# Eight-layer hybrid model on one Trainium2 core: attention divided inside its own block, and all products of the fast-weights layer on VectorE

## What is computed

```python
# a: alibi attention, 4 sequences of 1024 tokens, 16 heads of 8 values
scores = einsum('bqhd,bkhd->bhqk', q, k) / sqrt(8) + slopes * -abs(i - j)
X += einsum('bhqk,bkhd->bqhd', softmax(scores), v) @ Wout + bout
# m0: mixture of 8 experts, twice:  z += sum_e combine_e * w2_e(silu(w1_e rms(z)))
# b: the same attention with another bias:  scores = q k / sqrt(8) * decay ** abs(i - j)
# m1: the experts again
# f: fast weights, 16 heads of 64, 4 steps of the recurrence over 1024 columns
q = elu(q) + 1; k = elu(k) + 1; q /= sum(q); k /= sum(k); beta = sigmoid(beta)
for k_t, v_t, q_t, b_t in steps:
    W = W + (b_t * (v_t - W k_t))[:, None] * k_t[None, :]
    out = W q_t
h = layer_norm(h + out @ W_o)
# l0: lora ffn      c: centred attention, softmax(xc xc^T) x, no weights      l1: lora ffn
```

## Time and profile before

| what | us |
|---|---|
| median of 3 runs (3472.40 to 3484.07) | 3475.57 |
| the profiled execution, and its span | 3491.22, 3489.5 |
| attention a: projection, the block, normalise, project_out | 15.8 to 89.7, 94.7 to 586, to 603, to 616.4 |
| m0 | 617.8 to 1118.8 |
| attention b: the same four | 1121.6 to 1209.7, 1215.7 to 1705.9, to 1723, to 1737 |
| m1 | 1738.6 to 2240.1 |
| f: norm, dots, values, norm | 2243 to 2264.5, 2265.8 to 2557.3, to 2770.6, to 2805.6 |
| l0 | 2806.6 to 2856 |
| attention c: split, the block, normalise | 2857.9 to 2916.5, 2922.7 to 3402, to 3420 |
| l1 | 3421.2 to 3478.9 |

### The profile page before, as it was taken

How to read it: one execution, slowest core, us unless ns; L and a number is a source line. 1 busy time by engine, 2 the same in 40 slices (tenths; PEclk the granted TensorE clock), 3 DMA queues, 4 the chain that set the end, 5 groups by cost and what they waited for, 6 DMA issues and landing times. The chain is left out here.

```text
span 3489.5 us, 54163 instructions
## 1 busy us (share of the span) xinstructions
PE 2953.6 (85%) x18300; PEld 1343.2 (38%) x18300; DVE 2203.5 (63%) x3764; ACT 2352.7 (67%) x3403; POOL 411.4 (12%) x245
## 2 busy tenths in 40 slices
PE   4888888899998498898899999787868656999997
PEld 2221223566665211111356666522236441111116
DVE  5777777677776777777767777677789862000004
ACT  5789987555454699999655544464624447999992
POOL 2000000000000400000000000065634320000002
PEclk8899999999999799999999999899979867999996
DMA  5433441000000634333100000000000004222210
GB/s 121 57 53 50 59 59 20 25 0 1 0 0 5 171 48 55 53 52 49 29 6 0 1 0 0 26 1 0 0 0 0 0 14 99 41 41 37 42 29 27
DMA packets 68365, 111.08 MB, mean 32 GB/s; under 512 B 10656, under 2 KB 22944, under 8 KB 67312
## 3 DMA queue, kind: packets, MB, share of 16 engines
q1 hardware_dynamic: 68176, 108.58, 18.4%
HBM read 80.85 MB, written 27.69 MB: 31 GB/s over the span
## 5 line engine op out<-in xcount | busy, mean ns | idle before, releaser
L1660 ACT ACTIVATE m_mix_hidden<-m_mix_up_ps 128x512 f32<-128x512 f32 x512 | 305.5, 597 | 294.5 <-PE m_mix_up_ps L1604 294.5
L935 ACT ACTIVATE b_direct_probs<-b_direct_s_ps 128x1024 f32<-128x1024 f32 x512 | 473.6, 1094 | 14.3 <-PE b_direct_o_ps L883 11.7
L1612 PE MATMUL m_mix_down_ps<-m_w,m_mix_hidden 128*128 128x128 f32 x4096 | 474.8, 276 | 0.0
L935 ACT ACTIVATE c_att_probs<-c_att_s_ps 128x1024 f32<-128x1024 f32 x512 | 470.3, 1219 | 5.9 <-PE c_att_o_ps L883 4.1
L1612 PEld LDWEIGHTS m_mix_down_ps<-m_w,m_mix_hidden 128*128 128x128 f32 x4096 | 467.2, 192 | 15.3 <-issue 15.3
L1604 PE MATMUL m_mix_up_ps<-m_mix_ZT,m_w 128*128 128x512 f32 x1024 | 470.5, 617 | 0.3 <-ACT m_mix_hidden L1660 0.3
L935 ACT ACTIVATE a_direct_probs<-a_direct_s_ps 128x1024 f32<-128x1024 f32 (+10 forms) x512 | 431.5, 939 | 56.1 <-DVE a_direct_s_ps L964 42.2
L964 DVE SCALAR_TENSOR_TENSOR a_direct_s_ps<-distance,slopes,a_direct_s_ps 128x512 f32<-128x512 f32 (+3 forms) x512 | 355.4, 732 | 121.8 <-PE a_direct_s_ps L863 119.1
L961 DVE TENSOR_TENSOR b_direct_s_ps<-b_direct_s_ps,distance 128x512 f32<-128x512 f32 x512 | 336.0, 695 | 141.1 <-PE b_direct_s_ps L863 140.8
L950 DVE COPY c_out_t<-c_att_o_ps 128x512 f32 x32 | 22.1, 692 | 465.4 <-PE c_att_o_ps L883 465.2
L883 PE MATMUL b_direct_o_ps<-b_direct_probs,v_cols 128*32 128x512 f32 x2048 | 274.4, 608 | 14.1 <-DVE b_out_t L950 13.1
(11 more groups left out here) (330 smaller groups left out, 3511.7 us busy)
## 6 DMA issues: line engine op xcount, KB each, us to landing
qk_parts<-b_qkv_parts SPq DMA_DIRECT2D x48, 256.0 KB, 3.1
qk_parts<-a_qkv_parts SPq DMA_DIRECT2D x24, 256.0 KB, 3.6
a_k_rows<-qk_parts SPq DMA_DIRECT2D x32, 192.0 KB
a_q_rows<-qk_parts SPq DMA_DIRECT2D x32, 192.0 KB
b_k_rows<-qk_parts SPq DMA_DIRECT2D x32, 192.0 KB
b_q_rows<-qk_parts SPq DMA_DIRECT2D x32, 192.0 KB
qk_parts<-c_split_parts SPq DMA_DIRECT2D x24, 256.0 KB, 3.0
c_k_rows<-qk_parts SPq DMA_DIRECT2D x32, 192.0 KB
```

Source lines behind the costliest of these rows:

```text
L935: act.activation(probs[:, J % 2, j, lo:hi], s_ps[:, slot(hg, n), lo:hi], ACT.Exp).then_inc(exped, 1)
L1612: last = pe.matmul(down_ps[:, t % 2, e, :], hidden[:, e * HALVES + h, t * P:(t + 1) * P], w["w2"][:, e * HALVES + h, :], start=(h == 0), s ...
L1660: act.activation(hidden[:, f, :], up_ps[:, f % UP_BANKS, :], ACT.Silu).then_inc(silu_done, 1)
```

## The change

**Attention.** `out_t` is gone. `take_sums` copies into `taken`, with room for two groups. SyncE moves each group's results by four DMAs of 8 rows x 1024 to `joined` (heads on partitions, tokens along) and the sums of its four heads to DRAM. Once a batch is complete, its 16 x 1024 sums are read back as a dense 128x128 (`gather`), VectorE inverts them (`invert`), SyncE writes them (`keep`) and reads them spread over 128 partitions, 512 KB (`spread_out`), and VectorE multiplies the batch's 128x1024 (`scale`). In VectorE's order, `invert` stands after unit 24 of group 1, `scale` after unit 24 of group 3, of the batch that follows. The loads for a group now wait for the third exponential of the group before the coming one instead of for its takes, and stand ahead of the moves in SyncE's queue. The last group is treated apart: TensorE spreads its sums (`spread_sums`), VectorE divides on the spot (`divide`), and its product with `Wout` comes as a second matrix product into the same bank. The output projection (`finish`) is part of the block: eight groups of four products, six of them copied by ScalarE and added to `X` by GpSimd, the last two added by VectorE. The bias of the output is added by GpSimd after each batch. `normalise` is gone from all three layers; the old `project_out` remains in another form in a branch that is not taken with these inputs.

**Dots.** The two halves become 16 rounds in a row, without a loop. All products are VectorE's, in eight pieces, one after each take. The sums of the first half are copied, turned (into a PSUM bank of their own) and stored during rounds 8 to 11.

**Values.** The products of steps 1 and 2 are VectorE's too (`weigh`), with one buffer each instead of two, and the adds to `H` are put in another order.

The core of the diff:

```diff
-def attend_transposed(nc, tag, V, operands, out_t, ident, table=None, slopes=None, span=None):
+def attend_transposed(nc, tag, V, operands, joined, ident, table=None, slopes=None, span=None, X=None, w_out=None,
+                      b_out=None, kept=None):
+    SCALE_AT = 24
+    EARLY = 2 * (BATCH - 1)
+    KNOWN = (HG - 1) * GH * HD
+    FINISHED = (0, 1, 2, 3, EARLY, 4, 5, EARLY + 1)
...
+            def move(b, hg, past=0):
+                sp.wait_ge(o_out, b * (2 * HG) + (2 * hg + 6 - past * 2 * HG))
+                at = bass.ds(b * SEQ - past * SEQ, SEQ)
+                for j in range(GH):
+                    to = slice((hg * GH + j) * HD, (hg * GH + j + 1) * HD)
+                    sp.dma_start(joined[to, at], taken[VW * j:VW * j + HD, hg % 2, :]).then_inc(moved[hg % 2], 16)
+                sp.dma_start(sums_dram[bass.ds(b * HEADS + (hg * GH - past * HEADS), GH), :],
+                             taken[HD:P:VW, hg % 2, :]).then_inc(sums_kept[hg % 2], 16)
...
             def ahead(b, hg):
-                sp.wait_ge(o_out, b * (2 * HG) + (2 * hg + 2))
+                sp.wait_ge(exped, b * NB + ((hg - 1) * UNITS + SLOTS))
                 operands.load(sp, hg % HG, b + hg // HG)
...
+            def batch(b, first, final):
                 for hg in range(1, HG + 1):
-                    ahead(b, hg)
+                    if not (final and hg == HG):
+                        ahead(b, hg)
+                    if hg >= 2:
+                        move(b, hg - 2)
+                    elif not first:
+                        move(b, HG - 1, 1)
+                    if not first and hg >= 2:
+                        (gather, keep, spread_out)[hg - 2](b)
...
+            def scale(b, last=0):
+                dve.wait_ge(moved[0], b * (2 * MOVES) + 2 * MOVES)
+                dve.wait_ge(moved[1], b * (2 * MOVES) + (2 - last) * MOVES)
+                dve.wait_ge(spread, b * 16 + 16)
+                n = (HEADS - last * GH) * HD
+                out = joined[0:n, bass.ds(b * SEQ, SEQ)]
+                dve.tensor_tensor(out, out, inverse[0:n, :], ALU.mult).then_inc(scaled, 1)
+            def divide(c):
+                dve.wait_ge(sums_spread, c + 1)
+                held = taken[:, (HG - 1) % 2, c * BANK:(c + 1) * BANK]
+                dve.reciprocal(o_ps[:, c, :], o_ps[:, c, :]).then_inc(spread_inverted, 1)
+                dve.wait_ge(spread_inverted, c + 1)
+                dve.tensor_tensor(held, held, o_ps[:, c, :], ALU.mult).then_inc(divided, 1)
...
+                        if not first and n == SCALE_AT and hg == 1:
+                            invert(b - 1)
+                        if not first and n == SCALE_AT and hg == HG - 1:
+                            scale(b - 1)
+                            if final:
+                                invert(b, 1)
...
-    POOLS = (("kk", 1), ("kq", 0), ("kq", 1), ("kq", 3))
-    DVES = (("kk", 2), ("kk", 3), ("kq", 2))
+    PIECES = (("kk", 1, 0, 1), ("kq", 0, 0, 1), ("kq", 1, 0, 2), ("kk", 2, 0, 2), ("kk", 3, 0, 3), ("kq", 2, 0, 3),
+              ("kq", 3, 0, 2), ("kq", 3, 2, 4))
+    PIECES_AFTER = ((0, 1), (2,), (3,), (4,), (5,), (6,), (7,), ())
+    TURN_AT = {(FT8 + 1, 3): 0, (FT8 + 2, 1): 1, (FT8 + 2, 7): 2}
...
+            for r in range(ROUNDS):
+                for u in range(UNITS):
+                    take(r, u)
+                    if r:
+                        for piece in PIECES_AFTER[u]:
+                            multiply(r - 1, piece)
+                    if (r, u) in STORE_AT:
+                        store(0, STORE_AT[r, u])
...
-                    for t, prod in ((1, prod1), (2, prod2)):
-                        pool.wait_ge(v_out, b * STEPS + (t + 3))
-                        pool.tensor_tensor(heads(prod[:, half, :, :]), heads(v[:, half, 0:t + 1, :]),
-                                           of_tile(b, t, t + 1), ALU.mult).then_inc(scaled, 1)
...
+                def weigh(t, prod):
+                    dve.wait_ge(v_out, b * STEPS + (t + 3))
+                    dve.tensor_tensor(heads(prod[:, :, :]), heads(v[:, half, 0:t + 1, :]), of_tile(b, t, t + 1),
+                                      ALU.mult).then_inc(scaled, 1)
+                    dve.wait_ge(scaled, b * 3 + t)
```

509 lines of the change are left out of this document (301 added, 208 removed).

## The result

The median of four runs of the changed kernel is 3402.14 us (3391.58 to 3405.85), that of the kernel before, with one more run, 3479.82. The ratio is 0.9769 (95% interval 0.975 to 0.9787): 77.7 us less, where 87.5 were forecast. The base has moved too: the forecast was set from 3475.57, the median of three runs. The time lies 14 us above the forecast's value, in its range and just inside the forecast's own one (3372 to 3404).

What follows compares the result with a forecast made beforehand. No engine was busy throughout, so each stage had its own limit: ScalarE's exponentials in attentions a and b, VectorE and GpSimd products delaying each other in dots and values. Terms summed to -87.5 us: 3388 from a 3475.57 median, range 3362 to 3416.

Steps and rivals of the forecast that it cites:

- Dots: Dots of the fast-weights layer: all products on VectorE, no stop between halves, no loop; 233.8 us in place of 275.5, -41.7.
- the round: One round of dots: TensorE and VectorE level, 14.3 us taken where it was 16.33.
- Values: Combination of values: all products on VectorE, a tile of 19.1 us, seven periods 133.7 for 153.9; -19 us.
- The tails: Ends of attentions a, b and c: rounds of transpose, reciprocal, multiply and the projection removed; -16.9, -16.9 and -5.3 us.
- The waits at the multiplies: Inside attentions a and b: VectorE's added reciprocals and multiplies, and waits for the spread; +9 and +5.8 us, c 0.
- Loads ahead: Attention a: loads start some 7 us earlier, sparing TensorE's wait for a row of biases; -2.5 us, bounds 0 and -3.
- the third rival: Attentions a and b: the spread lands 8 us late at each multiply, 32 us more; 3420 us, chance 0.15.
- I give back 0.8 for the new clearings and copies at the block's start and its longer end: Attention a, taken alike for b: 0.8 us subtracted from the tail's gain of 17.7, leaving 16.9.
- its 26.8: The attention's share of the forecast gain in us: tails, loads ahead and the costs inside a and b together.
- TensorE's rounds at 15.6: Rival in dots: TensorE paces the rounds, banks handed back 0.16 later per take, 20 us back; 3408 us, chance 0.15.
- the rival without waits, 3375: Attentions a and b: the spread lands in time, so they lose some 2 us together; 3375 us, chance 0.15.
- The queue per group: Rival in a and b: DMA traffic exceeds 30.3 us per group, so every group waits; 3480 us, chance 0.02.

Runs made afterwards that it cites:

- second and third experiments: Changed kernel with the loads issued later, at the takes 3466.8 us or by five units 3443.1; and with the spread queued ahead of the load, 3391.1 us.
- twelve further traces: Traces of kernels with the old or the new attention, besides the profiled executions before and after; the unchanged l1 lasts 48.6 to 51.9 us in them.
- two comparisons of medians: New attention alone against the kernel before: 9.5 us less; changed kernel against the kernel before with new dots and values: 13.2 us less.
- the first experiment: Kernel before with the new dots and values, old attention: 3415.3 us; the other way round, with the new attention alone: 3470.1 us.
- the third, fourth and sixth experiments: Changed kernel with spread ahead of load, 3391.1 us; reciprocal and multiply after unit 30, 3396.2; loops written out, VectorE's 3399.0, TensorE's 3391.8, both with unit 30 3378.6.
- the fastest kernel here: Changed kernel with VectorE's and TensorE's batches written out, and reciprocal and multiply after unit 30: 3378.6 us, ratio 0.9712.

## Why the prediction was right, and where not

**Dots, forecast -41.7, measured -47.9.** The mechanism and both neighbours are as told: the products have the lengths of the earlier trace rows without GpSimd, and TensorE and VectorE are level. The term that was mis-sized is the round: 14.03, not 14.3. I had given each engine 0.3 for the other's waits, and they cost nothing. Fifteen rounds make 4 us of it. The stores cost 2.7 (three rounds of 14.9), for which 3.4 were set. The remaining 1.5 us of the difference are not assigned.

**Values, -19 and -18.5.** Seven periods are 135.3 us (2526.5 to 2661.8), where 133.7 were worked out; the tile is 19.2 for 19.1.

**The tails, -16.9, -16.9, -5.3 and -17.7, -17.6, -5.4.** Right in size and in their parts: 13.9 us after the last take, where 13.8 were added up, with the two reciprocals at 3.37 for 3.35.

**The waits at the multiplies, +9 in a and +5.8 in b.** The mechanism was right, as the second and third experiments show, and the waits were smaller than forecast: 2.9 us in three waits in a for 6.0 in two, 1.5 for 2.4 in b. The price of the multiplies stayed inside its bounds; what took b to +14.6 came from elsewhere, as told below. In c VectorE waited up to 7.8 us for the spread and nobody for VectorE: c's exponentials took 476.1 us for 476.2, as forecast.

**Loads ahead, -2.5.** Wrong as a price of the edit. I set it against the old kernel's one wait, and the group did get shorter (31.9 to 30.4). Within the new attention the early load is worth 65 us, because everything about the sums queues behind it. The sum held only because its landing times already had the early load in them; the two are not separate gains. The forecast did not cost the change without it, and the third rival (8 us at each multiply) is what that kernel does, at the gathers too: 3467.

**Missing: the jump back, and the entry of a.** This is the step that failed: "I give back 0.8 for the new clearings and copies at the block's start and its longer end", with nothing at all for the edges between the batches. In b a wait of 8.5 us stands where 0.6 were. And the first exponential of a comes 4.2 us after the block's first instruction where it took 1.4 (94.4 to 98.6, 94.7 to 96.1). The entry is not a jump: written-out batches leave it (4.9 to 5.6 us). In the twelve further traces it takes 3.8 to 8.4 us with the new attention and 1.4 and 3.1 with the old; its cause is open. Together the two are about 11 us. Smaller ones come on top: ScalarE's gap at the other edges of b is 1.7 and 1.9 us where it was 0.6 to 0.7, and went with ScalarE's loop written out, and the group behind TensorE's jump in a takes 33.2 us for 30.7. They are most of what the attention lacks in its 26.8: 9.5 and 13.2 us were measured in the two comparisons of medians.

That the two traces still show 22.4 us for the attention is due to the base. The traced execution of before had its groups of a 5.0 us longer than the same code had in the first experiment (487.5 and 482.5), those of b 0.9 and those of c 2.8. A sum made against that trace credits the change with these 9 us.

The rivals: TensorE's rounds at 15.6 did not come. With waits of 4.4 us in all, where 8.4 were forecast, the truth lay between the forecast and the rival without waits, 3375, and the jump hid it. The queue per group is not full: the DMA share rose from 0.39 to 0.44 in a and from 0.37 to 0.42 in b. The range held, and its value was 14 us too low; that it came so near owes something to errors that cancel, the round too long in the sum and the edges not in it.

Some sums of the prediction are off by a little: the round comes to 13.98 and not 13.96, the bound for rounds of 14.16 to -43.8 and not -45, 3416.1 for c is 5.1 less and not 5.3, and the traffic from which on the result is slower comes to 33.0 us a group and not 33.4. For the 200 KB/us that bounds the spread's speed from above no row of before is shown. None of this moves the forecast by a microsecond.

What caused the waits at the edge is shown as far as this: they stand at the jump of VectorE's or TensorE's loop and go when it is written out; the old attention, with loops of its own, has at most 2.6 us there in a and b (TensorE, in a); they do not need a load, since 5.1 us stand where none runs; and instruction packets come in at that time. That the engine waits for just these packets is the reading that fits, and is not shown: the trace names no releaser. Why the old loop's jump is free, and that of the same loop in a of the changed kernel, was not settled. A pass of VectorE's loop has 287 instructions in the trace where it had 282, which is all that the code shows.

Not tried: written-out batches with the multiply back at unit 24 in the last batch only, or with the spread ahead of the load. By an estimate from the rows of the third, fourth and sixth experiments this would take the 4.2 to 4.5 us off each of the two tails, some 8 us below the fastest kernel here, 3378.6 (ratio 0.9712).

## What to carry to other kernels

Before work is moved to GpSimd to relieve VectorE, look at whether VectorE's instructions with both inputs in SBUF get longer beside it: if they do, the two take turns, and it is cheaper to give all to VectorE, in pieces between the instructions that others wait for. A small transfer on which an engine will wait belongs ahead of a large load in the same queue: what it costs is the time of whatever is queued before it. After a change to the body of a hardware loop, look at the first instructions behind the jump for an idle time laid to "issue"; writing the loop out for all engines that jump at that point is the test.

## What the runs showed of the hardware

- At a jump back an engine can be idle for 4 to 9 us of "issue", VectorE (8.8, 5.8) as well as TensorE (3.96), and at the jump of the same loop in another layer for 0.6. With no load running VectorE's gap was 5.1 and 5.2 us, with one 5.8 to 8.8.
- A two-input product in SBUF took 4.02 us beside a GpSimd instruction of 4.0 and 1.22 alone, and a take with an input in PSUM 0.68 in both cases. Four additions a round that nobody waits for, 16 us of GpSimd, made the round 12 us longer.
- The same stage at the end of the program ran at a granted clock of 0.62 and of 0.80 in two executions, 57.7 and 48.4 us. A trace's own stages have to be compared with a second trace before a few microseconds in them are put down to a change.
